# A selective state-space scan on one Trainium2 core: from scans along time to steps of time

## The chip, the cores and the metric

The kernel runs on one core of one Trainium2 chip. A core has five engines that go by their own instruction queues: PE (TensorE, matmuls from SBUF into PSUM), DVE (VectorE), ACT (ScalarE), POOL (GpSimd) and SP, which here only issues DMAs. They wait for each other by semaphores. The metric is the device time of one execution in microseconds, lower is better.

## The reference

The kernel is a chain of layers on x of shape (16, 256, 256): a low-rank conditioned layer, a block with two selective state-space branches (forward and backward weights), and two transformer blocks. The change concerns the state-space branches. For each branch r, batch b, inner channel d (512) and state s (64) it computes

```
dt = softplus(xs @ xproj_w[:, :512] + dt_bias);  B, C = xs @ xproj_w[:, 512:]
A  = -exp(A_log)                                  # (512, 64)
h[t] = h[t-1] * exp(dt[t] * A) + (dt[t] * xs[t]) * B[t]      # state (d, s)
y[t] = sum over s of h[t] * C[t]
```

over 256 time steps t. u stands for dt * xs. That is 2 x 16 x 512 x 64 states over 256 steps.

## The kernel before

Four stages follow one another, with a barrier between: `conditioning` (small), `prepare` (xs, dt, u, B, C for 8 units of two batches, written to DRAM as three bf16 parts each), `scan`, and `finish_scan` with two `transformer` stages.

Partitions of the scan hold (b, s): two batches times 64 states. It goes through 64 sequences (branch, 128 channels, unit), each in 4 tiles of 64 time steps. `h` is a tile [128 partitions, 128 channels, 65 times], and `decay` a ring of three pieces of it. For each tile:

- PE makes A * dt into `s_pa` (`adt`, line 1226: K = 18 rows, weights A, 64 columns of dt; the 18 rows are the pairs of bf16 parts) and u * B into `s_pb` (`bu`, line 1245: 128 columns). A strip of 32 rows of the array holds one operand set, and neighbouring matmuls alternate between two strips.
- ACT takes exp of `s_pa` into `decay` (line 1352, 1024 elements) and copies `s_pb` into `h` (`take_bu`, line 1314, 1024 elements).
- DVE runs four `tensor_tensor_scan` along time over 2080 elements (line 1430): 32 channels times 65, in which a decay of 0 starts each channel anew.
- PE sums over s (`ch`, line 1258): the weights are C, set in a matrix of zeros `s_cz` of 32 columns per group, and the moving columns are the states of one time, 65 floats apart; four column groups write four strips of `s_py`. The result is transposed (line 1266) and stored.
- POOL fills `s_cz` with C (line 1385) and clears start columns (line 1392).

The order on each engine is written out by hand: PE repeats u B, A dt, y eight times per tile; ACT alternates exp and copy. SP loads all operands of a tile two tiles ahead. The first tile's operands are loaded within `prepare` (`first_tile`).

## Time and profile before

| | |
|---|---|
| median of 2 runs | 7788.3 us (7785.21 to 7791.39) |
| span of the profiled execution | 7785.8 us |
| prepare and conditioning | 0 to 864.7 us |
| scan | 864.7 to 5431 us |
| finish_scan and transformers | 5431 to 7785.8 us |
| busy over the span: PE, DVE, ACT, POOL | 87%, 78%, 75%, 25% |

The profile is of one execution. Its span runs from the first to the last instruction. The share of busy time is an average over stages with different limits, so each stage is read for itself. An instruction's mean time counts its whole duration, also where it overlaps with the one before it on the same engine.

### The profile page before, as it was taken

To read this page: it belongs to the slowest core of one execution; us is meant where nothing else is said; L and a number is where in the kernel's file an instruction comes from. 1 tells how busy PE (TensorE), PEld (TensorE's weight loads), DVE (VectorE), ACT (ScalarE), POOL (GpSimd) and SP (SyncE) were. 2 spreads that over 40 slices of the span, in tenths; PEclk is the share of its full clock that TensorE was granted. 3 is DMA by queue.
4 is the path that set the end of the run, shared out by engine and by line. 5 is a ranking of instruction groups with operands and counts; after the bars stand their busy time and mean duration, and the time that the engine had idled before them with its cause. 6 is when DMAs were issued, how large, how long until landed. Compare 5 with 4: busy or idle time off the path is not lost. (4 is left out here: it accounts for less than half of the span.)

```text
span 7785.8 us, 230318 instructions
## 1 busy us (share of the span) xinstructions
PE 6767.1 (87%) x93480; PEld 3552.4 (46%) x93480; DVE 6075.5 (78%) x3804; ACT 5841.4 (75%) x8254; POOL 1947.6 (25%) x983
## 2 busy tenths in 40 slices
PE   6888688888888888888888888887989999978888
PEld 3434344444444444444444444444335455444444
DVE  2555799999999999999999999998435444345554
ACT  3555699999999999999999999997225344345554
POOL 1111122222222212221222222222003223133333
PEclk8999799999999999999999999999999999989999
DMA  6666522222222222222222222222620000000000
GB/s 191 149 153 156 120 70 66 69 69 69 66 69 69 67 69 69 69 66 68 69 69 67 67 70 69 66 69 74 225 97 6 9 9 9 3 32 12 12 12 6
DMA packets 621669, 540.95 MB, mean 69 GB/s; under 512 B 490880, under 2 KB 529408, under 8 KB 607040
## 3 DMA queue, kind: packets, MB, share of 16 engines
q1 hardware_dynamic: 614400, 524.52, 23.4%
q8 instruction: 753, 12.34, 0.7%
q14 instruction: 308, 2.52, 0.1%
q10 hardware_dynamic: 6208, 1.57, 0.1%
HBM read 380.46 MB, written 145.49 MB: 68 GB/s over the span
## 5 line engine op out<-in xcount | busy, mean ns | idle before, releaser
L1430 DVE TENSOR_TENSOR_SCAN s_h<-s_decay,s_h 128x2080 f32<-128x2080 f32 x1024 | 4540.3, 4510 | 6.4 <-ACT s_decay L1352 5.3
L1314 ACT COPY s_h<-s_pb 128x1024 f32<-128x1024 f32 x2044 | 2511.8, 1229 | 53.0 <-PE s_pb L1245 41.4
L1258 PE MATMUL s_py<-s_h,s_cz 128*32 128x128 f32 x32768 | 2512.3, 436 | 4.3 <-DVE s_h L1430 4.2
L1352 ACT ACTIVATE s_decay<-s_pa 128x1024 f32<-128x1024 f32 x2048 | 2168.1, 1059 | 89.6 <-DVE s_h L1430 57.1
L1385 POOL TENSOR_TENSOR s_cz<-s_cl,s_one 128x128 f32<-128x128 f32 x256 | 905.4, 3537 | 3347.9 <-PE s_py L1258 3335.9
L1258 PEld LDWEIGHTS s_py<-s_h,s_cz 128*32 128x32 f32 x32768 | 1032.0, 122 | 468.0 <-issue 4.5
L2207 ACT ACTIVATE t_prob<-t_ps,t_nmax 128x256 f32<-128x256 f32 x1024 | 479.5, 482 | 275.7 <-DVE t_nmax L2348 274.8
L1226 PE MATMUL s_pa<-az,s_al 18*128 18x64 bf16 x16384 | 424.6, 192 | 299.3 <-ACT s_decay L1352 247.9
L1226 PE MATMUL s_pa<-s_dl,s_al 18*128 18x64 bf16 x16384 | 423.6, 191 | 287.0 <-ACT s_decay L1352 274.4
L1969 POOL TENSOR_TENSOR t_prob<-t_prob,t_rinv 128x512 f32<-128x512 f32 x512 | 528.7, 1039 | 508.4 <-DVE t_rinv L2342 508.4
L1226 PEld LDWEIGHTS s_pa<-az,s_al 18*128 18x128 bf16 x16384 | 302.6, 94 | 470.0 <-ACT s_decay L1352 434.6
L1226 PEld LDWEIGHTS s_pa<-s_dl,s_al 18*128 18x128 bf16 x16384 | 301.4, 94 | 461.4 <-ACT s_decay L1352 455.4
L2348 DVE TENSOR_REDUCE t_nmax<-t_ps 128x2 f32<-128x512 f32 x512 | 347.5, 682 | 174.7 <-PE t_ps L2029 172.3
L1245 PEld LDWEIGHTS s_pb<-s_ul,s_bl 18*128 18x128 bf16 x8192 | 235.2, 94 | 530.2 <-ACT s_h L1314 445.1
L1245 PEld LDWEIGHTS s_pb<-az 18*128 18x128 bf16 x8160 | 234.7, 94 | 507.5 <-ACT s_h L1314 442.4
L1245 PE MATMUL s_pb<-s_ul,s_bl 18*128 18x128 bf16 x8192 | 415.3, 221 | 26.0 <-issue 21.0
L1245 PE MATMUL s_pb<-az 18*128 18x128 bf16 x8160 | 413.9, 221 | 8.0 <-ACT s_h L1314 6.9
L2044 PE MATMUL t_ps<-t_ident,t_prob 128*128 128x128 f32 x2048 | 281.9, 280 | 43.0 <-ACT t_probt L2214 24.4
L2008 PE MATMUL t_ps<-t_h,t_wqkv 128*128 128x512 f32 x640 | 294.5, 605 | 12.0 <-DVE t_h L2268 12.0
L2029 PE MATMUL t_ps<-t_k,t_q 64*128 64x256 f32 x2048 | 292.3, 407 | 8.9 <-ACT t_prob L2207 8.9
L1392 POOL TENSOR_TENSOR s_h<-s_zcol,s_one 128x128 f32<-128x128 f32 x64 | 291.6, 4556 | 0.1
L2044 PEld LDWEIGHTS t_ps<-t_ident,t_prob 128*128 128x128 f32 x2048 | 221.4, 142 | 137.8 <-issue 75.0
(254 smaller groups left out, 6341.6 us busy)
## 6 DMA issues: line engine op xcount, KB each, us to landing
s_al<-A SPq DMA_DIRECT2D x256, 144.0 KB
az<-B SPq DMA_DIRECT2D x512, 72.0 KB
az<-U SPq DMA_DIRECT2D x512, 72.0 KB
az<-D SPq DMA_DIRECT2D x512, 72.0 KB
s_bl<-B SPq DMA_DIRECT2D x512, 72.0 KB
s_ul<-U SPq DMA_DIRECT2D x512, 72.0 KB
s_dl<-D SPq DMA_DIRECT2D x512, 72.0 KB
D<-p_dp SPq DMA_DIRECT2D x64, 384.0 KB, 6.5
```

Source lines behind the costliest of these rows:

```text
L1226: mm = pe.matmul(pa[j % 2][:, FG // 2 * bank + i, :], al[z][r:r + ROWS, d, :], dl[e % 2][r:r + ROWS, d, :], start=True, stop=True)
L1245: mm = pe.matmul(out, bl[e % 2][r:r + ROWS, t, :], moved, start=True, stop=True)
L1258: mm = pe.matmul(py[e % 2][QR * q:QR * q + QR, 0:P], cz[e % 2][:, l * P + QR * q:l * P + QR * q + QR], states, start=(l == 0), stop=(l == ...
L1314: act.copy(out, pb[:].rearrange("p b t d -> p d b t")).then_inc(bu_done, count)
L1352: act.activation(decay[(z + e + at) % RING][:, part, 1:W], pa[j % 2][:], ACT.Exp).then_inc(exp_done, 1)
L1385: pool.tensor_tensor(out, cl[e % 2][:].rearrange("p (l q) b -> p l q b", q=4), one[:, None, None, 0:1].to_broadcast([P, LROWS, 4, PAIR]), ...
L1430: dve.tensor_tensor_scan(seg, decay[(z + e + j) % RING][:].rearrange("p d w -> p (d w)"), seg, 0.0, ALU.mult, ALU.add).then_inc(scanned, 1)
L1969: pool.tensor_tensor(prob[at][:], prob[at][:], rinv[at][:, :, None].to_broadcast([P, 2, T]), ALU.mult).then_inc(s["norm"], 1)
L2008: mm = pe.matmul(ps[:, qkv.bank(name), :], wqkv[:, k, at:at + P], h1[:, k, :], start=(k == 0), stop=(k == FC - 1))
L2044: mm = pe.transpose(ps[:, SR + n % 2, kb * T + e * P:kb * T + (e + 1) * P], prob[n % RING][:, e, kb * P:(kb + 1) * P], ident[:])
L2207: op = act.activation(prob[at][:, b, :], ps[:, n % SR, b * T:(b + 1) * T], ACT.Exp, bias=nmax[at][:, b:b + 1], accum_out=rsum[at][:, b:b + 1])
L2348: dve.tensor_reduce(nmax[n % RING][:], ps[:, n % SR, :].rearrange("p (a t) -> p a t", t=T), axis=AX.X, op=ALU.max, negate=True).then_inc(s ...
```

## The change

The scan goes by time steps. There are four sweeps (branch and half of the channels), each through all 256 times. The state is [128 partitions (b, s), 8 units, 256 channels] = 2048 floats per partition, in four chunks of 512 (k = 0 to 3; a chunk is one PSUM bank and two units v). At each step:

- Chunks 0 and 1 live in PSUM (`s_pA`): DVE multiplies them in place by the decay (`times`), PE adds u B onto them by a matmul that accumulates (`to_a`), and ACT copies them to SBUF (`copy_a`) for y and the next product.
- Chunks 2 and 3: POOL multiplies the state in SBUF by the decay (`decayed`), PE makes u B in `s_pB` (`to_b`), and DVE adds both into SBUF (`plus`).
- y of the step before is 8 matmuls of 256 adjacent columns, into 32 rows each (`y`, halves v = 0 and 1). Both halves stand in one place of PE's queue, after `to_a` of chunk 1 and before the second A dt of the step (`produce`), but for step 1 of 16, where y goes last. y of 16 steps gathers in one bank and is then transposed.
- The decays for 8 steps are made while the other 8 are used, in two buffers: per step two bursts of 16 matmuls of A dt (`produce`) and four exps of 512 (`take_pair`). The matmuls write three banks in turn. A matmul reads 64 columns (8 times, 8 units) of dt of one channel, which are 64 bf16 numbers apart in the tile; an exp reads PSUM across 8 such matmuls and writes runs of 8 channels.
- C is set into `s_cz` by POOL twice in 16 steps, where it was once in a tile.

`prepare` computes dt by tokens in place of channels, transposes xs in place of u, and forms u on DVE (`take_u`), to write D, U and B in rows of time; y is read back from a layout of its own. The first tile is no longer loaded ahead.

The core of the diff:

```diff
                 def store_dt(i, r):
                     wait(sp, s["dp2"], 2 * i + r + 1)
                     for m in range(IC):
-                        sp.dma_start(scratch["D3"][r, m, i].rearrange("j b c d t -> d (j b c) t"),
-                                     dp[:, m].rearrange("p j (k t) -> p (j k) t", t=TS)).then_inc(s["dp_out"], 16)
+                        for h in range(2):
+                            at = P * m + TS * h
+                            sp.dma_start(scratch["D"][2 * r + m // 2, 2 * (m % 2) + h, :, :, i].rearrange(
+                                "a (k p) d -> p (a k) d", p=P),
+                                         dp[:, :, :, at:at + TS].rearrange("p j k d -> p (j k) d")
+                                         ).then_inc(s["dp_out"], 16)
...
-                def to_dt(i, r, columns):
+                def to_dt(i, r, tiles):
                     wait(pe, s["xs_done"], 2 * i + r + 1)
-                    for m in columns:
+                    for q in tiles:
                         for k in range(IC):
-                            mm = pe.matmul(g0[:, m, :], xp_w[r][:, k, m * P:(m + 1) * P], xs[r][:, k, :],
+                            mm = pe.matmul(g0[:, q, :], xs[r][:, k, q * P:(q + 1) * P], xp_w[r][:, k, 0:DI],
                                            start=(k == 0), stop=(k == IC - 1))
-                    if IC - 1 in columns:
+                    if 3 in tiles:
                         mm.then_inc(s["dt_mm"], 1)
...
+                def take_u(i, r, some=range(4)):
                     n = 2 * i + r
+                    wait(dve, s["dt_done"], n + 1)
+                    wait(dve, s["up0"], n)
+                    wait(dve, s["ures"], n)
                     for q in some:
-                        wait(dve, s["up0"], 4 * n + q + 1)
-                        dve.tensor_tensor(ur[:, q, :], g1[:, q % 2, :], up[:, 0, q, :], ALU.subtract).then_inc(s["ures"], 1)
+                        wait(dve, s["ut_mm"], 4 * n + q + 1)
+                        dve.tensor_tensor(u[:, q, :], g1[:, q % 2, :], dt_[:, q, :], ALU.mult).then_inc(s["u_done"], 1)
...
-                def ch(k, e, at, h):
-
-                    if h == 0:
-                        wait(pe, scanned, HALVES * (k + 1))
-                        wait(pe, c_filled, k + 1)
-                        wait(pe, y_done, k - 1)
-                    for bank in range(2):
-                        l = times(h, bank) // 4
-                        for q in range(4):
-                            states = hb[at][:, :, 1 + 4 * l + q].rearrange("p (a q i) -> p q a i", a=Q, q=Q)
-                            mm = pe.matmul(py[e % 2][QR * q:QR * q + QR, 0:P],
-                                           cz[e % 2][:, l * P + QR * q:l * P + QR * q + QR],
-                                           states, start=(l == 0), stop=(l == LROWS - 1))
+                def adt(p, w, banks):
+
+                    wait(pe, taken, 2 * p - 1)
+                    for i in range(8):
+                        for e in range(2):
+                            q, d = 2 * (w[1] % 2) + e, 8 * (w[1] // 2) + i
+                            mm = pe.matmul(pa[:, banks[e], DS * i:DS * (i + 1)],
+                                           al[QR * q:QR * q + ROWS, d, :],
+                                           dl[w[0]][QR * q:QR * q + ROWS].rearrange("p t i d -> p (t i) d")[:, :, d],
+                                           start=True, stop=True)
+                    mm.then_inc(filled, 1)
+
+                def bu(out, k, x, first, signal):
+
+                    j, t = x // TU, x % TU
+                    r = slice(QR * k, QR * k + ROWS)
+                    for v in range(2):
+                        mm = pe.matmul(out[:, HALF * v:HALF * (v + 1)], bl[j % 2][r, t, v, :], ul[j % 2][r, t, v, :],
+                                       start=first, stop=True, skip_group_check=not first)
+                    mm.then_inc(signal, 1)
+
+                def to_a(n, x, k):
+                    wait(pe, mul, 2 * n + k + 1)
+                    bu(pA[:, k, :], k, x, False, bu_a)
+
+                def to_b(n, x, G, k):
+
+                    if k == 2 and x % TU == 0:
+                        uses = 2 * G + x // (2 * TU) + 1
+                        wait(pe, u_in[x // TU % 2], UQ * uses)
+                        wait(pe, b_in[x // TU % 2], BQ * uses)
+                    wait(pe, added, 2 * n - 3 + k)
+                    bu(pB[:, k - 2, :], k, x, True, bu_b)
+
+                def y(n, x, v):
+
+                    if v == 0:
+                        wait(pe, copied, 2 * n + 2)
+                        wait(pe, added, 2 * n + 2)
+                    at = 34 * x if x < 8 else 36 * (15 - x) + 2
+                    for k in range(CH):
+                        mm = pe.matmul(py[QR * k:QR * (k + 1), HALF * v:HALF * (v + 1)],
+                                       cz[:, 2 * k + v, at:at + QR], hs[k][:, x % 2, HALF * v:HALF * (v + 1)],
...
+                def produce(G, x, w, head, first_of):
+                    of = x // TB
+                    if x % TB == 0 and w == 0:
+                        wait(pe, d_in[1 - of], DQ * (G + 1 + of))
+                    if w == 0 and x % 2 == 0 and of and first_of is not None:
+                        wait(pe, a_in[x % TB // 2], first_of)
+                    adt(pair(G, x, w, head), (1 - of, 2 * (x % TB) + w),
+                        [slot_bank(0, w, x, head, e) for e in range(2)])
...
+                def body(G, made, first, last, head, turn):
+                    for x in range(BODY):
+                        n = BODY * G + x
+                        more = not (last and x >= TB)
+                        late = x == 1
+                        before = (x - 1) % BODY
+                        has = not (head and x == 0)
+                        to_a(n, x, 0)
+                        if more:
+                            produce(G, x, 0, head, turn)
+                        to_a(n, x, 1)
+                        if has and not late:
+                            if x == 2:
+                                wait(pe, c_filled, 2 * G + 1)
+                            if x == 9:
+                                wait(pe, c_filled, 2 * G + 2)
+                            y(n - 1, before, 0)
+                            y(n - 1, before, 1)
+                        if more:
+                            produce(G, x, 1, head, turn)
+                        if not (last and x == BODY - 1):
+                            to_b(n + 1, (x + 1) % BODY, G + (x + 1) // BODY, 2)
+                        if not (last and x == BODY - 1):
+                            to_b(n + 1, (x + 1) % BODY, G + (x + 1) // BODY, 3)
+                        if late:
+                            wait(pe, ytok_done, G)
+                            wait(pe, c_filled, 2 * G + 1)
+                            for v in range(2):
+                                y(n - 1, before, v)
+                        if x == 2 and not head:
+                            turn_y(15 + 33 * G + 6, G, [(12 + e) % BANKS for e in range(2)])
...
+                def take(p, at, i, bank, w):
+
+                    q, d = 2 * (at % 2) + i, 8 * (at // 2)
+                    act.activation(
+                        dec[w][:].rearrange("p t i d -> p (t i) d")[:, :, DS * q + d:DS * q + d + 8],
+                        pa[:, bank, :].rearrange("p (d c) -> p c d", d=8), ACT.Exp).then_inc(taken, 1)
...
+                def copy_a(n, x, k):
+                    wait(act, bu_a, 2 * n + k + 1)
+                    act.copy(hs[k][:, x % 2, :], pA[:, k, :]).then_inc(copied, 1)
+
+                def take_pair(G, x, w, head):
+                    p = pair(G, x, w, head)
+                    wait(act, filled, p + 1)
+                    for e in range(2):
+                        take(p, 2 * (x % TB) + w, e, slot_bank(0, w, x, head, e), 1 - x // TB)
...
+                def body(G, made, first, last, head, turn):
+                    for x in range(BODY):
+                        n = BODY * G + x
+                        more = not (last and x >= TB)
+                        copy_a(n, x, 0)
+                        if more:
+                            if x % TB == 0:
+                                wait(act, mul, 2 * n)
+                                wait(act, added, 2 * n)
+                            take_pair(G, x, 0, head)
+                        copy_a(n, x, 1)
+                        if more:
+                            take_pair(G, x, 1, head)
+                        if x == 2 and not head:
+                            turned_y(15 + 33 * G + 6, G, [(12 + e) % BANKS for e in range(2)])
...
+                def decayed(n, x, k):
+                    wait(pool, added, 2 * n - 3 + k)
+                    m = of_chunk(k, x)
+                    pool.tensor_tensor(m, two(hs[k][:, (x + 1) % 2, :]), m, ALU.mult).then_inc(m_done, 1)
+
+                def body(G, made, first, last, head, turn):
+                    for x in range(BODY):
+                        n = BODY * G + x
+                        dec_ready(pool, G, x, head)
+                        if not (first and x == 0):
+                            decayed(n, x, 2)
+                            decayed(n, x, 3)
...
-                            if e and j % (HALVES // 2) == 0:
-                                wait(dve, carried, 2 * ((NT - 1) * n + e - 1) + j // (HALVES // 2) + 1)
-                            wait(dve, exp_done, STEPS * k + STRIDE * (j + 1))
-                            rows = slice(STRIDE * FG * j, STRIDE * FG * (j + 1))
-                            seg = hb[to][:, rows, :].rearrange("p d w -> p (d w)")
-                            dve.tensor_tensor_scan(seg, decay[(z + e + j) % RING][:].rearrange("p d w -> p (d w)"),
-                                                   seg, 0.0, ALU.mult, ALU.add).then_inc(scanned, 1)
-
-                sequences(dve, sequence)
-
-    keep["early"].close()
+                def times(n, x, k, first):
+                    wait(dve, copied, 2 * n + k - 1)
+                    if first:
+                        dve.memset(pA[:, k, :], 0.0).then_inc(mul, 1)
+                    else:
+                        state = two(pA[:, k, :])
+                        dve.tensor_tensor(state, state, of_chunk(k, x), ALU.mult).then_inc(mul, 1)
...
+                def plus(n, made, x, k, first):
+                    wait(dve, bu_b, 2 * n + k - 1)
+                    if k == 2:
+                        wait(dve, y_mm, 2 * n - 2)
+                    out = two(hs[k][:, x % 2, :])
+                    if first:
+                        dve.tensor_copy(out, two(pB[:, k - 2, :])).then_inc(added, 1)
+                    else:
+                        wait(dve, m_done, made + 2 * x + k - 3)
+                        dve.tensor_tensor(out, two(pB[:, k - 2, :]), of_chunk(k, x), ALU.add).then_inc(added, 1)
...
+                def body(G, made, first, last, head, turn):
+                    for x in range(BODY):
+                        n = BODY * G + x
+                        start = first and x == 0
+                        dec_ready(dve, G, x, head)
+                        for k in range(2):
+                            times(n, x, k, start)
+                        if x == 1 and not head:
+                            take_y(G)
+                        for k in range(2, CH):
+                            plus(n, made, x, k, start)
...
-                        sp.dma_start(y[r][:, m, :].rearrange("p (b t) -> p b t", b=PAIR), scratch["Y"][r, m, n]
-                                     ).then_inc(s[f"y_in{r}"], 16)
+                        sp.dma_start(y[r][:, m, :].rearrange("p (b t) -> p b t", b=PAIR),
+                                     scratch["Yt"][IC * r + m, :, bass.ds(PAIR * n, PAIR)]).then_inc(s[f"y_in{r}"], 16)
```

PE in the middle of the scan, before. The names: `s_pb` takes u B, `s_pa` A dt, `s_py` y; a REGISTER_ALU or ISA row belongs to a wait.

```order
L1226 MATMUL s_pa<-az,s_al 128x64 x16
L1258 MATMUL s_py<-s_h,s_cz 32x128 x8
L79 REGISTER_ALU
L1245 MATMUL s_pb<-s_ul,s_bl 128x128 x8
L1226 MATMUL s_pa<-az,s_al 128x64 x16
L1258 MATMUL s_py<-s_h,s_cz 32x128 x8
L79 REGISTER_ALU
L1245 MATMUL s_pb<-s_ul,s_bl 128x128 x8
```

PE in the middle of a body after, one whole step (`s_pA` and `s_pB` take u B for chunks 0, 1 and 2, 3; the operands of u B lie in the memory named `az`):

```order
L1239 MATMUL s_pA<-az 128x256 x2
L79 ISA
L1228 MATMUL s_pa<-s_dl,s_al 128x64 x16
L79 REGISTER_ALU
L1239 MATMUL s_pA<-az 128x256 x2
L1263 MATMUL s_py<-s_hs,s_cz 32x256 x8
L79 ISA
L1228 MATMUL s_pa<-s_dl,s_al 128x64 x16
L79 ISA
L1239 MATMUL s_pB<-az 128x256 x4
L79 REGISTER_ALU
```

y and A dt have kept their counts of 8 and 16 between waits. y has twice the columns and stands between the two bursts of A dt, with single pairs of u B around them; a step holds two bursts of A dt and one y, where three rows before repeated one of each.

ACT before, exp and copy in turn:

```order
L1352 ACTIVATE s_decay<-s_pa 128x16x64
L79 REGISTER_ALU x2
L1314 COPY s_h<-s_pb 128x128x2x4
L79 REGISTER_ALU
L1352 ACTIVATE s_decay<-s_pa 128x16x64
L79 REGISTER_ALU x2
```

ACT after:

```order
L1344 COPY s_hs<-s_pA 128x512
L79 REGISTER_ALU
L1338 ACTIVATE s_dec<-s_pa 128x64x8 x2
L79 REGISTER_ALU
L1344 COPY s_hs<-s_pA 128x512
L79 REGISTER_ALU
L1338 ACTIVATE s_dec<-s_pa 128x64x8 x2
```

Each copy out of `s_pA` is followed by two exps of half the size; copies for chunks 2 and 3 are gone.

DVE before:

```order
L1430 SCALAR_TENSOR_TENSOR s_h<-s_decay,s_h 128x2080
L79 REGISTER_ALU x2
L1430 SCALAR_TENSOR_TENSOR s_h<-s_decay,s_h 128x2080
L79 REGISTER_ALU
L1430 SCALAR_TENSOR_TENSOR s_h<-s_decay,s_h 128x2080
```

DVE after, at a change of the decay buffer (the REGISTER_ALU row on top, which the other steps don't have, belongs to the added wait for the last exp):

```order
L79 REGISTER_ALU
L79 ISA
L1437 TENSOR_TENSOR s_pA<-s_pA,s_dec 128x512 x2
L79 REGISTER_ALU x3
L1448 TENSOR_TENSOR s_hs<-s_pB,s_dec 128x512
L79 REGISTER_ALU x2
L1448 TENSOR_TENSOR s_hs<-s_pB,s_dec 128x512
```

Every scan has given way to two products in PSUM and two sums into SBUF per step.

## Rows read from the trace of the kernel before

**Rows 1.** Busy time by stage; columns: stretch, length, engines, PEclk, DMA share, GB/s.

```profile
core 0: us, PE busy (x) PEld busy (x) DVE busy (x) ACT busy (x) POOL busy (x), PEclk, DMA share, GB/s
0.00:864.73 864.73, 659.35 (x1992) 315.63 (x1992) 409.91 (x498) 436.50 (x461) 118.17 (x61) 0.91 0.68 164
864.73:5431.00 4566.27, 3968.98 (x82176) 2141.80 (x82176) 4545.51 (x1032) 4402.87 (x4990) 1198.46 (x325) 0.97 0.23 68
5431.00:7785.80 2354.80, 2138.79 (x9312) 1094.94 (x9312) 1120.09 (x2274) 1002.05 (x2803) 630.93 (x597) 0.96 0.11 38
```

**Rows 2.** Page, costliest groups, the scan; columns as busy, mean ns, idle.

```profile
L1430 DVE TENSOR_TENSOR_SCAN s_h<-s_decay,s_h 128x2080 f32<-128x2080 f32 x1024 | 4540.3, 4510 | 6.4 <-ACT s_decay L1352 5.3
L1314 ACT COPY s_h<-s_pb 128x1024 f32<-128x1024 f32 x2044 | 2511.8, 1229 | 53.0 <-PE s_pb L1245 41.4
L1258 PE MATMUL s_py<-s_h,s_cz 128*32 128x128 f32 x32768 | 2512.3, 436 | 4.3 <-DVE s_h L1430 4.2
L1352 ACT ACTIVATE s_decay<-s_pa 128x1024 f32<-128x1024 f32 x2048 | 2168.1, 1059 | 89.6 <-DVE s_h L1430 57.1
L1385 POOL TENSOR_TENSOR s_cz<-s_cl,s_one 128x128 f32<-128x128 f32 x256 | 905.4, 3537 | 3347.9 <-PE s_py L1258 3335.9
...
L1226 PE MATMUL s_pa<-az,s_al 18*128 18x64 bf16 x16384 | 424.6, 192 | 299.3 <-ACT s_decay L1352 247.9
...
L1226 PEld LDWEIGHTS s_pa<-az,s_al 18*128 18x128 bf16 x16384 | 302.6, 94 | 470.0 <-ACT s_decay L1352 434.6
...
L1245 PE MATMUL s_pb<-s_ul,s_bl 18*128 18x128 bf16 x8192 | 415.3, 221 | 26.0 <-issue 21.0
```

**Rows 3.** Scans on L1430; timeline at the start of the scan stage.

```profile
L1430 DVE TENSOR_TENSOR_SCAN s_h<-s_decay,s_h x1024: 4453/4461/4669, 876.6 to 5415.6; 128x2080 f32<-128x2080 f32 x171
...
864.92 0.67 PE L1226 MATMUL s_pa<-az,s_al 18*128 18x64 bf16 x26 [30.21 <-PEq L85]
...
866.31 1.14 ACT L1314 COPY s_h<-s_pb 128x1024 f32<-128x1024 f32 x1
...
869.39 0.40 POOL L1385 TENSOR_TENSOR s_cz<-s_cl,s_one 128x128 f32<-128x128 f32 x1
```

**Rows 4.** ACT in the scan; columns: start us, us, instruction.

```profile
2011.26 1.06 ACT L1352 ACTIVATE s_decay<-s_pa 128x1024 f32<-128x1024 f32 x1
2012.17 1.28 ACT L1314 COPY s_h<-s_pb 128x1024 f32<-128x1024 f32 x1
2013.20 1.17 ACT L1352 ACTIVATE s_decay<-s_pa 128x1024 f32<-128x1024 f32 x1
2014.38 1.24 ACT L1314 COPY s_h<-s_pb 128x1024 f32<-128x1024 f32 x1
2015.48 1.01 ACT L1352 ACTIVATE s_decay<-s_pa 128x1024 f32<-128x1024 f32 x1
```

**Rows 5.** ACT instructions of 512 elements out of PSUM.

```profile
L2214 ACT COPY t_probt<-t_ps 128x512 f32<-128x512 f32 x256 | 150.5, 588 | 47.4 <-PE t_ps L2044 47.4
...
L803 ACT ACTIVATE p_sz<-p_g 128x512 f32<-128x512 f32 x64 | 36.8, 597 | 88.0 <-PE p_g L661 87.9
```

**Rows 6.** DVE with one operand in PSUM; POOL with two in SBUF.

```profile
L1744 DVE TENSOR_TENSOR f_prod<-f_ps,f_gate 128x512 f32<-128x512 f32 x32 | 22.1, 690 | 47.6 <-PE f_ps L1617 47.4
...
L567 POOL TENSOR_TENSOR p_u<-p_dt,p_xs 128x1024 f32<-128x1024 f32 x32 | 90.4, 2846 | 276.2 <-DVE p_dt L966 276.2
L1955 POOL TENSOR_TENSOR t_q1h<-t_h 128x512 f32<-128x512 f32 x16 | 20.2, 1266 | 437.8 <-ACT t_h L2155 437.8
```

**Rows 7.** POOL: min/median/max of two lines.

```profile
L1385 POOL TENSOR_TENSOR s_cz<-s_cl,s_one x256: 399/3905/4337, 869.4 to 5407.0; 128x128 f32<-128x128 f32 x128
...
L1969 POOL TENSOR_TENSOR t_prob<-t_prob,t_rinv x512: 1036/1039/1042, 5845.4 to 7727.0; 128x512 f32<-128x512 f32 x171
```

**Rows 8.** PE bursts, in the scan and in the second attention.

```profile
3003.03 0.41 PE L1226 MATMUL s_pa<-az,s_al 18*128 18x64 bf16 x16 [0.24 <-ACT s_decay L1352]
3003.37 1.21 PE L1258 MATMUL s_py<-s_h,s_cz 128*32 128x128 f32 x16
3004.51 0.40 PE L1245 MATMUL s_pb<-s_ul,s_bl 18*128 18x128 bf16 x8
...
7103.68 1.07 PE L2071 MATMUL t_ps<-t_probt,t_v 128*32 128x256 f32 x16
7104.68 1.14 PE L2029 MATMUL t_ps<-t_k,t_q 64*128 64x256 f32 x8
```

670 lines of the change are left out of this document (291 added, 379 removed).

## The prediction

> **What bounds the kernel now.** I read the table of stages first. The scan stage lasts 4566 us of 7786, and in it DVE is busy for 4546; ACT has 4403, PE 3969, POOL 1198 [rows 1]. The groups of instructions say what fills DVE: 1024 scans of 2080 elements at 4.51 us [rows 2]. Their first and last starts are 876.6 and 5415.6, so one follows another every 4.44 us [rows 3]. A scan covers 2048 real elements per partition, which is also what one time step of the changed kernel covers (4 chunks of 512), and both kernels have 1024 of these portions. So the question is whether a step takes less than 4.44 us. ACT is close behind DVE already: 2044 copies of 1.23 us and 2048 exps of 1.06 us in that stage [rows 2]. A kernel that only freed DVE would gain some 4% of the stage. The change must also take work from ACT, and it does: half of the states (chunks 2 and 3) go by POOL and DVE and are not copied by ACT.
>
> **DVE.** The scans go. Four tensor_tensor of 512 elements come in per step, each with one operand in PSUM. The nearest row is 0.690 us [rows 6]: 4 x 0.69 = 2.76 us. Once in 16 steps a copy of 512 from PSUM comes on top (0.04 per step). The two products write PSUM, which no row shows. I take the same price; bounds are 2.5 (the scans also start some 0.05 before the one ahead ends) and 3.1.
>
> **POOL.** Two products of 512 per step with two operands in SBUF. Rows: 1.266 us for 512, and 2.846 for 1024, so 1.42 for 512 [rows 6]. That is 2.53 to 2.85 us, and I take the first, whose size is the same. The filling of C comes twice in 16 steps. It has a median of 3.9 us beside the scans, but 0.40 at its shortest, which is the one at 869 us before any scan ran [rows 3, 7]. The scans hold POOL back, and they are gone; I take 0.40, or 0.05 per step. POOL's chain stays inside the step: product, sum on DVE, product again is 1.27 + 0.69 + hand-overs, about 2.2 us.
>
> The Trainium skill (SBUF — State Buffer, section "Who interferes with whom") says that a DVE instruction with two inputs in SBUF shuts out a POOL instruction that reads SBUF, and that one with a single SBUF input does not. The trace agrees with the first half by the 3.9 against 0.40. The new DVE instructions have one input in SBUF each, so by this rule POOL's prices stand; the opposite case is a rival below.
>
> **ACT.** Per step 4 exps of 512 and 2 copies of 512, in place of one exp and one copy of 1024. A row of this size is 0.597 us for an activation and 0.588 for a copy, both out of PSUM [rows 5]. The exps now write runs of 8 elements. The copy of now, which writes runs of 4, takes 1.14 us when nothing else runs [rows 3]. An even 1024 at the pace of rows 5 and 2 (0.597 for 512, 1.059 for 1024) would be some 1.05, so I add 0.06 per exp (bounds 0 and 0.1). Back to back, instructions overlap: starts at 2011.26, 2012.17, 2013.20, 2014.38, 2015.48 against their durations give 0.15, 0.25, 0 and 0.14, on average 0.13 [rows 4]. So the sum is 4 x (0.597 + 0.06 - 0.13) + 2 x (0.588 - 0.13) = 3.03 us, with y's turning (4 small copies in 16 steps) 3.07. With no overlap it is 3.9.
>
> **PE.** Three kinds of work per step.
> y: 16 instructions (8 products in fp32) of 256 adjacent columns and 32 output rows. The attention has exactly this form: 16 of them from 7103.68 to 7104.68, 1.00 us [rows 8]. The y of now is 16 of 128 columns, 260 bytes apart, 1.14 us [rows 8]. Half as many instructions do the same: what takes two such bursts now, 2.28 us, takes one of 1.00.
> u B: four pairs of 256 columns in bf16, each pair in one strip of rows. Now 8 of 128 take 0.40 alternating over two strips [rows 8]. The granted clock is 0.97 of full speed in the scan [rows 1], the level of 2.4 GHz, at which 256 columns need 0.107 us, and the pair cannot alternate; with the weight load between I take 0.27 per pair, 1.08 in all (bounds 0.9, and 1.6 if each load of 0.094 [rows 2] stands open).
> A dt: two bursts of 16, as now (0.34 from 3003.03 to 3003.37 [rows 8]), but the moving columns of dt lie 128 bytes apart, now side by side. The only strided reads of the trace are those of y: 1.14/128 against 1.00/256 is 2.3 times as long per column. About 0.13 of each burst looks like a fixed part (16 x 64 columns over two strips at 2.4 GHz is 0.21 of the 0.34). I take 0.13 + 2.3 x 0.21 = 0.62 per burst, 1.24 per step. Bounds: 0.68 (stride free) and 2.2 (every column at the strided fp32 price: 1.14 less 0.15, times four strips, over 16 x 128, is 1.93 ns; 16 x 64 x 1.93 / 2 + 0.13 = 1.12 per burst).
> Sum 3.32 us, bounds 2.5 and 4.8.
>
> The Trainium skill (SBUF — State Buffer, section "Door 1: The DMA port swizzle", note on cachelines) says that a read stays at full rate only with further hits in the same line of 16 bytes. The trace agrees for fp32 by y's 2.3 times. The rule speaks against the new layout of dt, where each bf16 column opens a line; it gives no price for it.
>
> **What is not hidden.** The decays lie in two buffers of 8 steps. At each turn DVE's product waits for the last exp (the order shows an added wait there), and u B and ACT's copy wait for DVE. PE then stands for the pair of exps 1.13 + the product 0.69 + hand-overs 0.2 less its two u B of 0.54, some 1.5 us in 8 steps, 0.19 per step; ACT 0.69 + 0.27 + hand-overs 0.4, 0.17 per step. Behind the waiting product on DVE stand the sums of chunks 2 and 3, and behind PE's wait the A dt of the next exps. Once in 16 steps PE turns y, 8 instructions, about 1 us, 0.06. PE comes to 3.57 and ACT to 3.24. Both go in order, and A dt has three banks, so that PE is at most a pair ahead of the exps. For waits on each other I add 0.13, a choice and not a measurement: **3.7 us per step**.
>
> **Around the scan.** The first tile was loaded ahead of the barrier, and the first scan began 12 us after it (864.7 to 876.6 [rows 3]). Now A, dt, u, B arrive after it and 32 exps of 0.6 come first: some 30 us more, plus the last turn, 33 in all against PE's start. The step before the scan computes dt by tokens: as many matmuls, DVE and ACT instructions of the same sizes, POOL one subtraction of 2048 in place of two products of 1024 (2.85 each [rows 6]); I take 0, bounds -30 and +40. DMA: bytes stay, y is written in pieces of 64 bytes, 4096 in 16 steps. The share in the scan is 0.23 [rows 1] and has room.
>
> **Sum.** The profiled span, 7785.8, is within the runs (7785.2 to 7791.4, median 7788.3). 7788 - 4566 + 33 + 1024 x 3.7 = **7044 us**, 9.6% faster, a little under 7050.
>
> **Rivals.**
> A, slower: dt's strided columns cost their fp32 price. Then each burst takes 1.12 instead of 0.62, PE's step 3.57 + 1.0 + 0.13 = 4.7, and the time is 7788 - 4566 + 33 + 4813 = 8068. It decides from about 0.9 us per burst, where the step passes 4.3. For it: y's row is the only strided one. Against: bf16 has half the bytes, and there are two strips of 18 rows, not four strips of all 128. 0.12.
> B: ACT has no overlap, since nearly each of its instructions follows a wait. 3.9 + 0.17 + 0.13 = 4.2 us, 7556. For it: the 0 among the four gaps. Against: in today's scan it overlaps with as many waits. 0.13.
> C: stride is free for bf16. PE falls to 3.0, ACT's 3.24 with waiting decides, 3.4 us, 6737. 0.17.
> D: any DVE work shuts out POOL. They alternate, 2.76 + 2.53 = 5.3 us, 8680. Against: POOL's t_prob takes 1036 to 1042 ns in all its 512 runs while DVE is busy in PSUM [rows 7]. 0.03.
> The forecast, 3.5 to 4.0 us per step, has 0.55.
>
> **Numbers.** Forecast and C lie below 7632 (2% faster, about what a measurement of this kernel can tell from no change), and most of B: 0.82 faster. The rest of B and a mild A: 0.06 same. A and D: 0.12 slower. The range reaches from just under C over B's 7556: 6700 to 7650. A, D and the far ends of B and C stay outside.
>
> **What would show it.** In the new profile: PE and ACT both over 80% in the scan, DVE about 75%, POOL 70%; steps every 3.7 us; y bursts 1.0 us; A dt bursts 0.6 (A: over 0.9; C: 0.34); exps at 0.66 with starts 0.53 apart; POOL's products at 1.27 with no dependence on DVE; a gap of 1 to 1.5 us on PE and ACT at every eighth step. The prediction fails if a burst of A dt takes over 0.9 us, if POOL's product goes past 1.7, or if the hand-overs cost 0.5 rather than 0.13.

## The result, and the profile after

The changed kernel takes **8696.3 us** (median of 2 runs, 8694.6 to 8697.9) where the kernel before took 7788.3: 1.117 times as long, 95% interval 1.1145 to 1.1187. Forecast were 7044 us, with a range of 6700 to 7650. The profiled execution has a span of 8696.1 us.

The table of stages of the kernel after, in the columns of [rows 1]:

```profile
0.00:859.90 859.90, 661.64 (x2008) 317.49 (x2008) 387.08 (x540) 433.13 (x414) 92.87 (x45) 0.91 0.64 163
859.90:6330.00 5470.10, 4992.46 (x57552) 2733.96 (x57556) 2705.29 (x4156) 3274.60 (x6396) 2597.94 (x2171) 0.50 0.15 42
6330.00:8696.10 2366.10, 2143.66 (x9364) 1097.15 (x9356) 1122.95 (x2280) 1004.74 (x2809) 633.78 (x599) 0.96 0.11 38
```

The first and the last stage are nearly as before (864.7 and 2354.8 in [rows 1]; the cut at 6330 lies some 7 us ahead of the end of the scan). The scan stage grew from 4566 to 5470 us. DVE, which was idle for 21 us of it, is now busy for half; PE is busy for 91%. And the column that I did not question reads 0.50 instead of 0.97: TensorE's granted clock is at 1.2 GHz, not 2.4, in all of the scan stage.

The costliest groups on the page of the kernel after, which answer to [rows 2]:

```profile
L1408 POOL TENSOR_TENSOR s_dec<-s_hs,s_dec 128x512 f32<-128x512 f32 x2040 | 2548.8, 1272 | 2822.7 <-DVE s_hs L1448 1854.6
L1338 ACT ACTIVATE s_dec<-s_pa 128x512 f32<-128x512 f32 x4096 | 2223.4, 594 | 1828.1 <-PE s_pa L1228 1828.1
L1228 PE MATMUL s_pa<-s_dl,s_al 18*128 18x64 bf16 x32768 | 2211.7, 282 | 287.8 <-ACT s_dec L1338 230.2
...
L1437 DVE TENSOR_TENSOR s_pA<-s_pA,s_dec 128x512 f32<-128x512 f32 x2040 | 1405.2, 695 | 1334.7 <-ACT s_hs L1344 791.8
L1448 DVE TENSOR_TENSOR s_hs<-s_pB,s_dec 128x512 f32<-128x512 f32 x2040 | 1325.4, 686 | 1369.6 <-PE s_pB L1239 1176.7
L1263 PE MATMUL s_py<-s_hs,s_cz 128*32 128x256 f32 x16384 | 1978.6, 634 | 0.0
```

The prices of DVE, ACT and POOL are close to the forecast ones. What is new is in the right half, the idle time: ACT's exps waited 1828 us for A dt, and DVE's sums 1177 us for u B. PE sets the pace. Its timeline over one step and over one turn of the decay buffers (start, duration, instruction, idle time before and its releaser):

```profile
3000.61 1.93 PE L1263 MATMUL s_py<-s_hs,s_cz 128*32 128x256 f32 x16
3002.47 0.94 PE L1228 MATMUL s_pa<-s_dl,s_al 18*128 18x64 bf16 x14
3003.14 0.39 PE L1239 MATMUL s_pA<-az 18*128 18x256 bf16 x1
3003.24 0.29 PE L1228 MATMUL s_pa<-s_dl,s_al 18*128 18x64 bf16 x2
3003.33 0.42 PE L1239 MATMUL s_pA<-az 18*128 18x256 bf16 x1
3003.34 0.60 PE L1239 MATMUL s_pB<-az 18*128 18x256 bf16 x4
3004.22 1.05 PE L1228 MATMUL s_pa<-s_dl,s_al 18*128 18x64 bf16 x16 [0.27 <-ACT s_dec L1338]
3005.09 0.60 PE L1239 MATMUL s_pA<-az 18*128 18x256 bf16 x2
3005.62 1.93 PE L1263 MATMUL s_py<-s_hs,s_cz 128*32 128x256 f32 x16
...
3030.73 1.93 PE L1263 MATMUL s_py<-s_hs,s_cz 128*32 128x256 f32 x16
3032.59 1.05 PE L1228 MATMUL s_pa<-s_dl,s_al 18*128 18x64 bf16 x16
3033.47 0.61 PE L1239 MATMUL s_pB<-az 18*128 18x256 bf16 x4
3035.67 0.39 PE L1239 MATMUL s_pA<-az 18*128 18x256 bf16 x1 [1.59 <-DVE s_pA L1437]
```

A burst is a run of matmuls of one kind. Its duration overlaps with the next one, so its cost is the time from its start to the start of what follows: 0.87 for a burst of A dt (3004.22 to 3005.09) that lasts 1.05. From y to y a step takes 3005.62 - 3000.61 = 5.01 us: y 1.86, two bursts of A dt of 0.87 each, u B 1.14 beside them, and 0.27 of waiting. At a turn of the decay buffers PE stands idle for 1.59 us. Over some 750 steps from 1000 to 5000 us the mean is 5.33, and over all 1024 it is 5.30.

### The profile page after: what moved, and what is told of

Its sections match the earlier page's. It is cut to its first block and busy times, and to the rows that moved or that the text cites. A ratio compares the mean times of both kernels' runs of the same rounds, so it can differ in the third digit from the quotient of the medians.

```text
span 8696.1 us, 182764 instructions
## 1 busy us (share of the span) xinstructions
PE 7797.8 (90%) x68920; PEld 4148.6 (48%) x68920; DVE 4215.3 (48%) x6974; ACT 4712.5 (54%) x9618; POOL 3324.6 (38%) x2814
## 5 line engine op out<-in xcount | busy, mean ns | idle before, releaser
L1408 POOL TENSOR_TENSOR s_dec<-s_hs,s_dec 128x512 f32<-128x512 f32 x2040 | 2548.8, 1272 | 2822.7 <-DVE s_hs L1448 1854.6
L1338 ACT ACTIVATE s_dec<-s_pa 128x512 f32<-128x512 f32 x4096 | 2223.4, 594 | 1828.1 <-PE s_pa L1228 1828.1
L1228 PE MATMUL s_pa<-s_dl,s_al 18*128 18x64 bf16 x32768 | 2211.7, 282 | 287.8 <-ACT s_dec L1338 230.2
L1228 PEld LDWEIGHTS s_pa<-s_dl,s_al 18*128 18x128 bf16 x32768 | 1647.3, 116 | 1504.0 <-ACT s_dec L1338 773.8
L1437 DVE TENSOR_TENSOR s_pA<-s_pA,s_dec 128x512 f32<-128x512 f32 x2040 | 1405.2, 695 | 1334.7 <-ACT s_hs L1344 791.8
L1448 DVE TENSOR_TENSOR s_hs<-s_pB,s_dec 128x512 f32<-128x512 f32 x2040 | 1325.4, 686 | 1369.6 <-PE s_pB L1239 1176.7
L1263 PE MATMUL s_py<-s_hs,s_cz 128*32 128x256 f32 x16384 | 1978.6, 634 | 0.0
L1239 PE MATMUL s_pA<-az 18*128 18x256 bf16 x4096 | 1230.0, 401 | 204.1 <-DVE s_pA L1437 197.9
L1344 ACT COPY s_hs<-s_pA 128x512 f32<-128x512 f32 x2048 | 1213.2, 593 | 319.3 <-PE s_pA L1239 319.2
L1239 PE MATMUL s_pB<-az 18*128 18x256 bf16 x4096 | 619.1, 400 | 0.0
```

Of the source, the lines that this page charges most:

```text
L1228: mm = pe.matmul(pa[:, banks[e], DS * i:DS * (i + 1)], al[QR * q:QR * q + ROWS, d, :], dl[w[0]][QR * q:QR * q + ROWS].rearrange("p t i d - ...
L1239: mm = pe.matmul(out[:, HALF * v:HALF * (v + 1)], bl[j % 2][r, t, v, :], ul[j % 2][r, t, v, :], start=first, stop=True, skip_group_check=n ...
L1263: mm = pe.matmul(py[QR * k:QR * (k + 1), HALF * v:HALF * (v + 1)], cz[:, 2 * k + v, at:at + QR], hs[k][:, x % 2, HALF * v:HALF * (v + 1)], ...
L1338: act.activation(dec[w][:].rearrange("p t i d -> p (t i) d")[:, :, DS * q + d:DS * q + d + 8], pa[:, bank, :].rearrange("p (d c) -> p c d" ...
L1344: act.copy(hs[k][:, x % 2, :], pA[:, k, :]).then_inc(copied, 1)
L1408: pool.tensor_tensor(m, two(hs[k][:, (x + 1) % 2, :]), m, ALU.mult).then_inc(m_done, 1)
```

## The experiments

All times are of whole kernels; "clock" is the mean granted clock from 1000 to 5000 us, inside the scan. The kernel before ran beside each group, at 7778 to 7787 us and a mean clock of 0.96 every time. Warm once, y apart and the four kernels with a laid copy of dt were timed in three more rounds, the others once.

| run | built on | time, us | clock |
|---|---|---|---|
| y twice | after | 10147 | 0.58 |
| dense products | after | 9614 | 0.59 |
| warm once | after | 8701 | 0.50 |
| y strided | after | 8597 | 0.76 |
| y apart | after | 8218 | 0.50 |
| A dt adjacent | after | 7821 | 0.50 |
| adjacent, apart | after | 7472 | 0.50 |
| adjacent, apart, dense | after | 7712 | 0.67 |
| laid by DVE, apart | after | 8248 | 0.50 |
| the same, 4 dense | after | 8695 | 0.54 |
| the same, 6 dense | after | 8512 | 0.70 |
| laid by ACT, apart | after | 7957 | 0.50 |
| before, half of y | before | 7773 | 0.50 |
| before, y adjacent | before | 7921 | 0.50 |

### Does the clock merely stay where the scan found it?

The scan of the changed kernel starts at 0.50 and stays there. Perhaps its steps would hold a high clock if they found one. So 32 dense products (128 x 128) run once, ahead of the first step:

```diff
                 to_b(0, 0, 0, 3)
+                for _ in range(32):
+                    pe.matmul(py[:, 0:P], ident[:], ident[:], start=True, stop=True)
                 bodies(pe, body)
```

> Only addition: 32 fp32 products of 128 x 128 on PE into the still unused bank of y, once, behind the 16 pairs of A dt that come ahead of the first step (about 14 us). The changed kernel's scan runs wholly at a granted clock of 0.50, and it was 0.50 before the scan began. Theory 1 (the clock stays where it was at the start: what the steps do does not raise it, but would hold it up): the scan goes at 1.00 for good, the mean step of 5.30 us falls to about 3.7, the time is 7000 to 7400. Rival (the matmuls of a step cannot hold the clock up either): it is back at 0.50 within a few steps and the time is 8700 to 8720.

8701 us, ratio 1.118 (1.116 to 1.120): the rival's number. The windows of this run (columns as in [rows 1]) and PE's timeline in it:

```profile
908.00:912.00 4.00, 4.00 (x38) 4.00 (x37) 0.00 (x0) 0.00 (x0) 0.64 (x1) 1.00 0.19 80
912.00:916.00 4.00, 2.83 (x49) 2.12 (x49) 1.63 (x3) 2.93 (x6) 0.00 (x0) 1.00 0.04 18
916.00:920.00 4.00, 3.73 (x50) 2.39 (x50) 2.27 (x4) 3.43 (x7) 2.85 (x3) 0.57 0.02 4
920.00:924.00 4.00, 4.00 (x48) 1.74 (x40) 1.90 (x4) 2.15 (x4) 2.15 (x2) 0.50 0.21 33
```

```profile
914.13 0.93 PE L1228 MATMUL s_pa<-s_dl,s_al 18*128 18x64 bf16 x14 [0.70 <-ACT s_dec L1340]
915.00 0.39 PE L1239 MATMUL s_pB<-az 18*128 18x256 bf16 x4
```

The dense products brought the clock to 1.00, and the steps lost it again within two windows. The kernel before needs no such help. It too comes to its scan at 0.50, and its own matmuls raise the clock within 8 us:

```profile
900.00:904.00 4.00, 2.87 (x62) 1.92 (x58) 4.00 (x2) 4.00 (x5) 0.00 (x0) 0.50 0.07 15
908.00:912.00 4.00, 3.56 (x84) 1.89 (x80) 4.00 (x2) 4.00 (x5) 0.00 (x0) 1.00 0.20 69
```

The second thing to see is a price. At 914 us the clock is 1.00 and u B is quick (0.39 against 0.60), but 14 products of A dt take 0.93 us, the very time that they take at 0.50 (0.94 above). A dt over strided columns does not follow the clock.

### More work over all rows

```diff
                     at = 34 * x if x < 8 else 36 * (15 - x) + 2
+                    if v == 1:
+                        for k in range(CH):
+                            for h in range(2):
+                                pe.matmul(py[QR * k:QR * (k + 1), HALF * h:HALF * (h + 1)], none[:],
+                                          hs[k][:, x % 2, HALF * h:HALF * (h + 1)], ...)
```

> Every step does y's 8 products (16 instructions of 256 columns, all 128 rows) a second time, with weights of zero, so the result stays. If the clock is low because the steps now hold too little work over all rows, it goes to 1.00: the step is 3.3 + 1.0 + waits 0.4, some 4.7 us, 8100 to 8250 in all, which is faster with more work. If it stays at 0.50, each step takes 1.87 us more, 10600 in all.

```diff
+                    def dense():
+                        for h in range(2):
+                            pe.matmul(py[:, HALF * h:HALF * (h + 1)], none[:, 0:P], none[:, P:P + HALF], ...)
+                    if v == 1:
+                        dense()
...
                     mm.then_inc(y_mm, 1)
+                    if v == 0:
+                        dense()
```

> The changed kernel with 4 more products per step between the halves of y: 128 rows by 128 output columns, bf16, 256 moving columns each, weights of zero. If the clock follows how much of the array works, these raise it to 1.00 where y a second time reached 0.59: A dt's strided bursts stay 0.87, y 1.0, the step with the filler 3.98 + 0.43, 8050 to 8250 in all. If the clock stays at 0.50, each step takes 0.85 more: 9550.

Both raised the clock in parts only, and paid for it: 10147 and 9614 us. They do give the step's price at full clock. PE in the run with y twice, where the clock stood at 1.00 (L1266 is the added half):

```profile
3031.54 1.04 PE L1229 MATMUL s_pa<-s_dl,s_al 18*128 18x64 bf16 x16 [0.47 <-ACT s_dec L1345]
3032.41 0.39 PE L1240 MATMUL s_pA<-az 18*128 18x256 bf16 x2
3032.74 0.64 PE L1270 MATMUL s_py<-s_hs,s_cz 128*32 128x256 f32 x8
3033.19 1.08 PE L1266 MATMUL s_py<-s_hs,s_none 128*32 128x256 f32 x16
3034.06 0.65 PE L1270 MATMUL s_py<-s_hs,s_cz 128*32 128x256 f32 x8
3034.64 0.94 PE L1229 MATMUL s_pa<-s_dl,s_al 18*128 18x64 bf16 x14
...
3036.39 1.05 PE L1229 MATMUL s_pa<-s_dl,s_al 18*128 18x64 bf16 x16 [0.47 <-ACT s_dec L1345]
```

The step is 3036.39 - 3031.54 = 4.85 us. Less the added 0.87 (3033.19 to 3034.06) that leaves 3.98: A dt 2 x 0.87, y 1.03, waiting 0.47, u B the other 0.74. So the clock costs 5.01 - 3.98 = 1.03 us per step, about 1055 us in 1024 steps. This is an estimate: no run held the changed kernel at 1.00 throughout, and it takes the waiting to be the same without the added products.

### The stride of dt, and y's place

```diff
-   dl[w[0]][QR * q:QR * q + ROWS].rearrange("p t i d -> p (t i) d")[:, :, d],
+   dl[w[0]][QR * q:QR * q + ROWS].rearrange("p t i d -> p (t i d)")[:, DS * d:DS * (d + 1)],
```

> A dt reads 64 adjacent columns instead of 64 that lie 128 bytes apart (so it multiplies the wrong values of dt, and the output is not the reference's). At a clock of 0.50 a burst of adjacent columns took 0.61 us in the kernel before and takes 1.05 now. Theory (stride costs 0.44 per burst at 0.50): 0.88 us less per step, 7750 to 7850, if the clock stays at 0.50; if the denser steps also raise it to 1.00, 6800 to 7000. Rival (stride costs nothing, the 1.05 is a matter of the other instructions around): 8650 to 8700.

7821 us, 875 less, with the clock still at 0.50: the stride theory met its number (0.88 x 1024 = 901). A burst lasts 0.61 us instead of 1.05, as it did in the kernel before at this clock.

```diff
                             y(n - 1, before, 0)
-                            y(n - 1, before, 1)
                         if more:
                             produce(G, x, 1, head, turn)
+                        if has and not late:
+                            y(n - 1, before, 1)
```

> The second half of y goes behind the second pair's A dt instead of directly behind the first half. If the order within a step decides whether the clock rises, this shows another clock and a time below 7500. If PE is simply bound by its columns at 0.50, nothing changes: 8650 to 8750.

8218 us, ratio 1.056 (1.054 to 1.057). Neither expectation: the clock did not move, yet 478 us went. What PE waited for from 3000 to 4000 us, first in the kernel after, then with y apart (sum, times, longest):

```profile
PE s_pa L1228 <- ACT s_dec L1338: 40.3, 152, 0.3
PE s_pA L1239 <- DVE s_pA L1437: 36.0, 22, 2.5
```

```profile
PE s_pA L1239 <- DVE s_pA L1438: 13.0, 25, 1.7
PE s_pa L1228 <- ACT s_dec L1339: 7.9, 13, 0.6
```

With both halves of y in one place, 1.9 us of y stand between one pair's A dt and the other's, while on the other side the two pairs follow each other closer than ACT frees one of the three banks. With a half in each gap PE is busy 3910 of 4000 us instead of 3665. That is 4.85 us per step instead of 5.33; 0.34 of the difference is idle time (335 us in 751 steps against 90 in 824); the other 0.14 I put down to more overlap of u B with A dt, which the run doesn't show by itself. So the one place of y is itself a loss.

Both edits together:

> Both edits together: A dt reads adjacent columns (of wrong values), and y's second half goes behind the second A dt. Alone they gave -875 and -478 us. If they add up, 7340; if they share a cause (PE is the bound in both), less: 7400 to 7550. Clock still 0.50.

7472 us. Of the single gains of 875 and 478, together 1353, there remain 1224.

The same, with the dense products as above:

> Adjacent columns (of wrong values), y apart, and the 4 dense products, two with each half of y. If the clock is 1.00, neither stride nor clock is left, and the step is what the forecast said of the rest, 3.4 to 3.8 us: 6800 to 7150. If the clock stays at 0.50, some 0.85 per step on top of the run without the dense products: 8200.

7712: slower than without the dense products, since the clock comes and goes (mean 0.67). But its stretches at 1.00 show what a step costs with neither handicap. First PE's timeline, then windows of the next turn (columns as in [rows 1]):

```profile
3008.68 0.64 PE L1272 MATMUL s_py<-s_hs,s_cz 128*32 128x256 f32 x8
3009.25 0.39 PE L1266 MATMUL s_py<-s_none 128*128 128x256 bf16 x2
3009.61 0.41 PE L1229 MATMUL s_pa<-s_dl,s_al 18*128 18x64 bf16 x16
...
3011.64 0.64 PE L1272 MATMUL s_py<-s_hs,s_cz 128*32 128x256 f32 x8
```

```profile
3016.00:3020.00 4.00, 4.00 (x83) 1.68 (x83) 3.50 (x6) 4.00 (x9) 3.56 (x4) 1.00 0.02 7
3020.00:3024.00 4.00, 3.00 (x61) 1.19 (x56) 1.95 (x4) 3.28 (x7) 1.16 (x2) 1.00 0.14 37
3024.00:3028.00 4.00, 3.83 (x52) 1.69 (x56) 3.30 (x6) 2.66 (x6) 4.00 (x4) 0.62 0.22 79
```

The step takes 2.96 us, with some 0.7 of it dense products (each pair holds PE for 0.36, 3009.25 to 3009.61). ACT is busy for all 4.00 us of the first window, so at this pace it is at its limit too. In the last two rows the clock falls right after the window in which PE stood idle for 1.00 us at a turn; whether that idle time is what loses it is tried further down.

### What held the clock up before

In the kernel before, y is the matmul work with the longest bursts, and the change altered it most. First, half of its columns are left out:

```diff
+   cut = Q if l == 0 else Q // 2
-   mm = pe.matmul(py[e % 2][QR * q:QR * q + QR, 0:P],
+   mm = pe.matmul(py[e % 2][QR * q:QR * q + QR, 0:QR * cut],
                   cz[e % 2][:, l * P + QR * q:l * P + QR * q + QR],
-                  states, start=(l == 0), stop=(l == LROWS - 1))
+                  states[:, 0:cut], start=(l == 0), stop=(l == LROWS - 1))
```

> The kernel before, in which every product of y but the first of sixteen has 64 moving columns instead of 128 (half of y's columns are left out). Its scans, and all else, stay. Theory: it is the share of y, the one PE work that uses all 128 rows, in PE's time that holds the clock up. Then the scan's granted clock falls from 0.97 to about 0.50, and, since DVE sets the pace and PE still fits (2 x 0.61 + 2 x 0.60 + 2 x 0.6 = 3.6 us of 4.44), the time stays within 7780 to 7900. Rival (something else than y holds it, such as steadiness of the work): the clock stays above 0.9.

The theory's numbers: clock 0.50, time 7773 us. Next, y in the kernel before has all its columns, but reads adjacent ones:

> The kernel before, with y's products reading 128 adjacent columns of a constant tile (the identity, so the values of y are left out) in place of 128 states 260 bytes apart. As many products and as many columns, but a burst should take about half the time at full clock: 0.5 to 0.6 us instead of 1.21. Theory (the columns count: the array is granted its clock by the columns that pass over all rows): the clock stays at 0.97. Rival (the time counts in which PE works over all rows, which the slow strided reads stretched): it falls to 0.50, as it did with half of y's columns. The time stays near 7780 in both cases, since DVE sets it.

```diff
-   states = hb[at][:, :, 1 + 4 * l + q].rearrange("p (a q i) -> p q a i", a=Q, q=Q)
+   states = ident[:]
```

The changed kernel, in turn, gets strided reads of y:

> The changed kernel, with y's 256 columns read in an order of 16 bytes apart (the values of y land in other columns). As many columns, more time: 16 instructions about 2.3 us if such a stride costs what 260 bytes do (1.21 per 128), against 1.87 at a clock of 0.50. If the time of work over all rows counts, the clock rises, and u B gets shorter (0.39 to 0.28 per instruction): 8600 to 8800 in spite of the slower y. If columns count, it stays at 0.50: 9050 to 9150. If 16 bytes apart costs nothing, y stays at 1.93 and the time at 8700, clock 0.50.

```diff
-   hs[k][:, x % 2, HALF * v:HALF * (v + 1)],
+   hs[k][:, x % 2, HALF * v:HALF * (v + 1)].rearrange("p (a b) -> p b a", b=4),
```

The stretch 1000 to 5000 us of four kernels: before, before with adjacent reads of y, after, after with strided reads of y.

```profile
1000.00:5000.00 4000.00, 3490.16 (x72345) 1875.77 (x72345) 3996.83 (x903) 3879.64 (x4395) 1057.65 (x283) 0.97 0.23 68
```

```profile
1000.00:5000.00 4000.00, 3695.36 (x69986) 2489.23 (x69978) 3878.78 (x873) 3647.01 (x4251) 895.00 (x273) 0.50 0.22 66
```

```profile
1000.00:5000.00 4000.00, 3665.20 (x42217) 2006.25 (x42214) 1985.35 (x3049) 2399.55 (x4692) 1903.55 (x1589) 0.50 0.15 42
```

```profile
1000.00:5000.00 4000.00, 3558.57 (x42996) 1940.12 (x42990) 2019.91 (x3102) 2442.59 (x4774) 1958.34 (x1615) 0.76 0.15 43
```

Within each kernel the instructions and their columns are the same in number, and the clock follows how y is read. In the kernel before, y read strided columns (1.21 us per burst of 128 columns, [rows 8]). With adjacent ones the clock falls to 0.50, the burst lasts 1.08 there, and the kernel gets 133 us slower, since ACT's copies now wait for u B (325 of the 4000 us). In the changed kernel, strided reads lift the clock to 0.76 and make it 99 us faster. u B's products get shorter (326 to 333 ns instead of 401), although each burst of y is slower (1.93 before this edit, at the low clock) and hardly quicker where the clock is 1.00. Two bursts of that run, the first at 0.50 and the second at 1.00:

```profile
3000.90 2.02 PE L1263 MATMUL s_py<-s_hs,s_cz 128*32 128x256 f32 x16
...
3010.49 1.99 PE L1263 MATMUL s_py<-s_hs,s_cz 128*32 128x256 f32 x16
```

So the strided reads that the change did away with, which I booked as a pure gain, had kept the clock up. The run with adjacent reads took them from a constant tile, so other data is a second difference in it; the run on the changed kernel has the same data and shows the opposite step. Its clock stops at 0.76, short of the 0.97 of the kernel before; the stride and the matmuls around y are others there, and no run tells which of them makes that difference. Each of these runs was timed once; the two differences in time, 133 and 99 us, lean on that, the clocks much less. What the chip measures to come to this isn't known from these runs.

### A version that is faster than both?

To be adjacent, the right columns have to be made so: a step's 8 x 64 values of dt are copied into a small buffer, from which PE reads (y apart in all of these). First DVE copies:

```diff
+   dve.tensor_copy(dc[:].rearrange("p d c -> p c d"),
+       dl[part][:].rearrange("p t i d -> p (t i) d")[:, :, 8 * piece:8 * piece + 8]).then_inc(laid, 1)
...
-   dl[w[0]][QR * q:QR * q + ROWS].rearrange("p t i d -> p (t i) d")[:, :, d],
+   dc[QR * q:QR * q + ROWS, i, :],
```

> All of the computation, with both remedies: y's halves apart, and dt laid side by side for real: in each step DVE copies the 8 x 64 columns of dt that the step's A dt needs (512 bf16 elements of 128 partitions) into one small buffer, from which PE reads adjacent columns. DVE is busy 64% in the run with both edits on wrong values, so a copy of 0.3 to 0.6 us should be covered: 7450 to 7600, against 7472 there. If the hand-over PE, DVE, PE through the single buffer stalls PE instead, 0.5 us or more per step: over 7900. Clock 0.50.

Then ACT copies, reading with the stride instead of writing with it:

```diff
+   act.copy(dc[:], dl[part][:].rearrange("p t i d -> p d (t i)")[:, 8 * piece:8 * piece + 8, :]
+            ).then_inc(laid, 1)
```

> The kernel with y apart and dt laid side by side, but ACT does the copy, and the other way round: it reads columns 128 bytes apart and writes adjacent ones (DVE read runs of 8 and wrote 128 bytes apart, 1.44 us). ACT stands between PE and the exps anyway, so the single buffer needs no further wait. Theory (scattered 2-byte writes made DVE's copy slow): about 0.6 us, as ACT's other instructions of 512; ACT is then busy 3.0 + 0.6 = 3.6 of 3.9 us per step, and the time 7500 to 7700, faster than both kernels. Rival (strided access costs 2.5 ns per element on any engine and in both directions): the copy takes 1.3 or more, ACT sets the step at 4.4, over 8000.

The copy of 512 bf16 elements, from 3000 to 4000 us, on DVE, what PE waited for it, and the copy on ACT in the other run:

```profile
L1457 DVE COPY s_dc<-s_dl 128x512 bf16<-128x512 bf16 x204 | 294.6, 1444 | 0.4 <-issue 0.4
```

```profile
PE s_pa L1231 <- DVE s_dc L1457: 101.5, 177, 2.1
```

```profile
L1353 ACT COPY s_dc<-s_dl 128x512 bf16<-128x512 bf16 x218 | 230.5, 1057 | 0.0
```

DVE needs 1.44 us, PE waits 0.50 per step for it, and the time is 8248 us (ratio 1.060, 1.058 to 1.061): all of the stride's gain gone. ACT, which reads the strided columns and writes adjacent ones, needs 1.06, not 0.6; it is then busy for 3524 of 4000 us, and 7957 us is 1.022 times the kernel before (1.020 to 1.024). Per element that is 2.8 ns on DVE and 2.1 ns on ACT.

With DVE's copy, 4 or 6 dense products stand at y in each step, and 8 more at each turn:

```diff
+                        if x % TB == 0 and not (head and x == 0):
+                            dense(8)
                         to_a(n, x, 0)
```

> The same with 4 dense products per step (256 columns, 128 x 128, weights of zero) and 8 more at each turn of the decay buffers, where PE stands waiting and the clock was seen to fall. With 4 alone the clock was at 1.00 in stretches of some 15 us between turns, 0.65 on average, and the steps at 1.00 took 2.96 us. If the turn's idle time is what lets it fall, it now stays at 1.00: steps of 3.0 to 3.4, 6750 to 7150. If not, it stays near 0.65 and the time is above 7600.

> As the run before with 6 dense products per step: 0.21 us more PE work at full clock. If 4 are enough to hold it, this is up to 200 us slower than with 4; if 4 are not enough and 6 are, it is the faster of the two, 6900 to 7200.

They took 8695 us (clock 0.54 in the profiled execution, the longest of four that spread from 8622 to 8759) and 8512 us (clock 0.70). Filling the turn did not hold the clock. PE still waited for DVE's copy, 47 and 93 us of the 1000 from 3000 us on, so no run shows what the filling does for a PE that never waits. No version that computes the whole result beats the kernel before. The runs at 7472 and 7712 us do, but they multiply the wrong dt.

## Why the prediction was wrong, point by point

- **"The granted clock is 0.97 of full speed in the scan [rows 1], the level of 2.4 GHz"** is the step that failed. It was read from the scan of the kernel before and carried over to the changed one, though the change replaced the matmuls that ran there, and none of the rivals doubted it. The runs showed 0.50 in its place. At that clock y takes 1.86 us instead of 1.03 and u B 1.14 instead of 0.74: 1.23 per step, of which 0.20 comes back as less waiting (0.27 instead of 0.47).
- **"0.13 + 2.3 x 0.21 = 0.62 per burst" of A dt**: mis-sized. 0.87 at either clock, where the adjacent burst took 0.34 at full clock. That is 0.50 more per step than forecast. Rival A had the mechanism, at 1.12 per burst, and gave itself the decision only from 0.9 on: at 0.87 and nothing else wrong the step is 3.70 + 0.50 = 4.20 and the time 7556, still faster. The strided y in [rows 8] gave a time per column, but I scaled only the part above an assumed fixed share.
- **u B, "1.08 in all"**: 0.74 at full clock, 0.34 less than forecast and below the bound of 0.9. In the timeline pairs of u B run beside A dt (3003.14 to 3003.33); the sum had them one after another.
- **"For waits on each other I add 0.13"**: 0.27 at the low clock, 0.47 at the high one, close to the 0.5 that the prediction named as a sign of failure. It was called a choice, and it is a matter of y's place: with y apart PE waited for ACT 8 of 1000 us instead of 40.
- **The turn**, "0.19": the step over a turn is 6.46 (3030.73 to the next y at 3037.19), 1.45 more, 0.18 per step. Right. **y's turning**, "0.06": the four steps from 3030.73 to 3054.03 with a turn in them take 23.30. Less 4 x 5.01 and the 1.45, that leaves 1.81 in 16 steps, 0.11 per step.
- **DVE, ACT, POOL.** Products in PSUM 695 and sums 686 ns against 0.69; exps 594 ns against the forecast 0.66 us, and two in a row 1.09, so starts 0.50 apart against 0.53; POOL 1272 ns against 1.266 us, with C's filling at 0.40. Right, or a little dear for the exps, and rivals B and D fall: ACT overlaps, and POOL isn't shut out. The busy shares came out lower than forecast only since the step is longer: ACT 60%, DVE 49%, POOL 47%. The Trainium skill's rule (SBUF — State Buffer, "Who interferes with whom"), on which POOL's prices were said to stand, agrees with the 1272.
- **Around the scan.** The first A dt starts at 877.7 and the first step some 28 us later, about 46 us after the stage's start instead of 33; the stage before is 5 us shorter. The whole adds up: 860 + 46 + 1024 x 5.30 + 2359 behind the scan = 8692, against 8696.

The sum, per step: 3.70 forecast + 1.23 clock - 0.20 waiting that it hides + 0.50 stride - 0.34 u B + 0.34 waiting at full clock + 0.03 y + 0.04 turns and y's turning = 5.30, against 5.33 measured from 1000 to 5000 us and 5.30 over all steps. With the clock at 1.00 the step would be some 4.27 and the time 8696 - 1055 = 7641 us, by the estimate above: a little faster than before, just inside the range, and still 600 above the forecast. The clock decided the sign; stride and waiting took most of the gain that was left. The error on u B went the other way and hid a part of theirs, which was luck. Rival A's 8068 and D's 8680 lie nearer the result than the forecast, D's by chance, since its mechanism didn't occur.

**What speaks for the reading of PE alone as the bound**: taking work from PE (the adjacent columns) gives back 0.85 us per step of the 0.88 taken, where no other engine's work changes.

## What to carry to other kernels

TensorE's granted clock went with the kernel's own matmuls here, at 0.97 in one scan and 0.50 in the other on the same chip: before costing a change by prices at 2.4 GHz, ask which of PE's work stood in the stretch when the clock was high, and whether the change shortens it. A change that makes PE's main work quicker can lose the clock for all the rest. Where another engine was the bound this cost little or nothing (7773 us with half of y's columns, 133 us more with all of them); where the change made PE the bound it cost an estimated 1055 us, more than all of the gain. And a transposed layout had its price on each engine that met it: with 128 bytes between 2-byte elements PE paid 2.6 times the adjacent price at full clock (0.87 against 0.34), ACT 1.8 times (1.06 against 0.59) and DVE 2.1 times (1.44 against 0.68), the last two against even f32 copies of as many elements out of PSUM. Writing dt in the right order in the first place is the way left; no run here tried it.
